# A 64-batch stack of six attentions, an expert layer and a Mamba block on one core: the exponential moved behind the transpose, own scores copied out by ScalarE, and the expert fetches split

## The reference

```python
# L0: x += attn(ln(x), own, causal); x += attn(ln(x), ctx); x += gelu(ln(x) @ fc1) @ fc2
# L1: x += attn(ln(x), own);  x += attn(ln(x), ln(ctx));  x += top-2-of-8 experts(ln(x))
# L2: x += mamba2(rms(x));    x += attn(ln(x), ctx, mask_keys)
# L3: x = ln(x + attn(x, ctx, mask_pairs))
s = jnp.einsum('blhd,bmhd->bhlm', q, k)
p = jax.nn.softmax(s, axis=-1)
return jnp.einsum('bhlm,bmhd->blhd', p, v)
```

## Time and profile before

| what | value |
|---|---|
| median of 3 runs | 3734.92 us (3720.77 to 3736.32) |
| the profiled execution's own time | 3734.74 us |
| its span | 3732.9 us |
| PE busy | 3195.7 us, 86% |
| PEld busy | 2269.6 us, 61% |
| DVE busy | 2605.4 us, 70% |
| ACT busy | 2652.3 us, 71% |
| POOL busy | 1246.9 us, 33% |
| mean granted clock of PE | 0.952 |

### The profile page before, as it was taken

The page is one execution under the profiler, slowest core; times in us unless marked ns, Lnnn a source line. Parts: engine busy times, 40 slices in busy tenths (PEclk is TensorE's granted clock), DMA queues, the critical chain, the costliest instruction groups (busy, mean ns, idle before and its releaser), DMA issues.

```text
span 3732.9 us, 87645 instructions
## 1 busy us (share of the span) xinstructions
PE 3195.7 (86%) x30064; PEld 2269.6 (61%) x30064; DVE 2605.4 (70%) x5408; ACT 2652.3 (71%) x5088; POOL 1246.9 (33%) x1615
## 2 busy tenths in 40 slices
PE   6898888888888979998988888998888997777897
PEld 3566556566756657665665656666565665665565
DVE  7877787755477777556888777665888877326775
ACT  4777777777876757887776766788776776656566
POOL 3122333212153353112244244212235434214632
PEclk9999999999999989999999999999999998989899
DMA  7013200134410033221000014322000004442000
GB/s 280 1 43 135 109 6 15 30 97 108 103 37 3 18 100 89 69 64 43 19 22 14 3 44 109 83 72 57 26 23 20 6 19 108 103 112 59 16 2 13
DMA packets 211920, 212.98 MB, mean 57 GB/s; under 512 B 51808, under 2 KB 155168, under 8 KB 211232
## 3 DMA queue, kind: packets, MB, share of 16 engines
q1 hardware_dynamic: 203296, 190.58, 18.1%
q0 software_dynamic: 8192, 16.79, 1.5%
HBM read 135.98 MB, written 71.30 MB: 56 GB/s over the span
## 4 chain that ended last, share of the span: by engine, by line
PE 39%; DVE 23%; ACT 15%; issue 8%; SPq 7%; DMA 4%; POOL 4%; ACTq 0%; DVEq 0%; POOLq 0%
PE ps L1933 8%; DVE mx L2320 6%; PE ps L1923 5%; PE ps L1945 4%; DVE pr L2326 4%; DMA b_up<-cols 4%; ACT block_hid L2211 3%; ACT pt L2164 3%; PE ps L1892 3%; PE ps L1953 2%; PE ps L2005 2%; PE ps L1918 2%; DVE kx L2326 2%; ACT xh L2114 2%; SPq L1818 1%
## 5 line engine op out<-in xcount | busy, mean ns | idle before, releaser
L2320 DVE TENSOR_REDUCE mx<-ps 128x8 f32<-128x616 f32 (+1 forms) x704 | 671.4, 954 | 334.7 <-PE ps L1923 316.4
L2164 ACT ACTIVATE pt<-ps 77x512 f32<-77x512 f32 (+1 forms) x1408 | 768.9, 593 | 126.1 <-PE ps L1933 123.2
L2576 POOL TENSOR_TENSOR kx<-kT,in_tiles 128x308 f32<-128x308 f32 (+1 forms) x384 | 315.7, 822 | 830.5 <-PE ps L1923 740.0
L1933 PE MATMUL ps<-k_sb,pr 128*77 128x128 f32 (+1 forms) x3776 | 538.9, 284 | 33.9 <-ACT pr L2155 10.3
L1933 PEld LDWEIGHTS ps<-k_sb,pr 128*77 128x77 f32 (+1 forms) x3776 | 421.1, 147 | 142.2 <-issue 73.2
L1945 PE MATMUL ps<-pt,v 77*16 77x128 f32 (+2 forms) x11264 | 444.3, 278 | 29.0 <-ACT pt L2164 11.2
L2326 DVE TENSOR_TENSOR pr<-ps,mx 128x616 f32<-128x616 f32 (+1 forms) x472 | 450.3, 954 | 16.2
L2155 ACT ACTIVATE pr<-pr 128x616 f32<-128x616 f32 (+1 forms) x472 | 392.7, 840 | 75.6 <-DVE pr L2326 74.6
L2173 ACT ACTIVATE og<-ps 128x256 f32<-128x256 f32 x704 | 267.3, 381 | 236.8 <-PE ps L1945 233.6
L1923 PE MATMUL ps<-kx,qT 32*128 32x308 f32 (+2 forms) x2816 | 361.6, 547 | 42.2 <-ACT pt L2164 15.8
L1945 PEld LDWEIGHTS ps<-pt,v 77*16 77x16 f32 (+2 forms) x11264 | 251.8, 97 | 181.1 <-issue 85.1
(11 more groups left out here) (209 smaller groups left out, 5733.3 us busy)
## 6 DMA issues: line engine op xcount, KB each, us to landing
w_up<-weights SPq DMA_DIRECT2D x160, 256.0 KB
w_down<-weights SPq DMA_DIRECT2D x160, 256.0 KB
sent<-block_hid SPq DMA_DIRECT2D x42, 512.0 KB, 6.3
made<-block_hid SPq DMA_DIRECT2D x42, 512.0 KB, 6.3
block_rows<-sent SPq DMA_DIRECT2D x160, 64.0 KB
b_down<-expert_b SPq DMA_DIRECT2D x160, 64.0 KB
made<-block_out SPq DMA_DIRECT2D x160, 64.0 KB, 2.2
cT<-ctx_cols SPq DMA_DIRECT2D x32, 154.0 KB, 3.1
```

The source lines that it names most:

```text
L1933: i = tr(p[0:keys, j * L:(j + 1) * L], probs[s][pl.slot(unit, 3)][:, c:c + keys], ident)
L2164: go_act(pt[s][0:keys, q % 2, :], p[0:keys, :], ACT.Copy).then_inc(probsT_ready.sem, 1)
L2320: link(v_.tensor_reduce(m, tile, AX.X, ALU.max, negate=True))
L2576: tell(pool, g_.tensor_tensor(spread_keys[s][:, pl.slot(step, 2), 0:4 * keys].rearrange("p (h k) -> p h k", h=4), kT[s][:, b * keys:(b + 1 ...
```

## The change

Three things change in what runs, and a fourth in the order.

1. In all attentions the exponential is taken off `soft`. The shifted scores are transposed, and ACT's copy from PSUM to `pt` becomes an exponential (L2376 in the changed file). The instruction on 8x77 or 8x128 elements in SBUF (L2155) is gone.
2. In the two own attentions (`LIFTED = (0, 2)`) a step `lift` stands ahead of `soft`: ACT copies the unit's scores out of PSUM (L2366), DVE takes the maximum from SBUF. `soft` is then on POOL: scores plus negated maximum in place (L2811). In the context attentions DVE's two instructions stay.
3. Of a pair of expert blocks the rows are fetched by a step of their own (`fetch`, L2013), the first weights for each block apart (`take`, with j), each with its own semaphore; the second bias has its own semaphore too. `block_turn` of the next pair waits for the rows alone, and stands ahead of this pair's `block_down`. The register loads stand ahead of the waits. `b_up` has two buffers.
4. The planner's durations and all its preference tables are new, so all engines' orders differ.

```diff
@@ attention_steps, expert_steps
+            out += [("lift", a, s, *units[n])] if a in LIFTED else []
             out.append(("soft", a, s, *units[n]))
...
-    out = [("table", g), ("take", g, 0), ("take_down", g, 0)]
+    out = [("table", g), ("fetch", g, 0), ("take", g, 0, 0), ("take", g, 0, 1), ("take_down", g, 0), ("block_turn", g, 0)]
     for p in range(PAIRS):
-        out += [("block_turn", g, p), ("block_up", g, p, 0), ("block_up", g, p, 1)]
-        out += [("take", g, p + 1)] if p + 1 < PAIRS else []
+        more = p + 1 < PAIRS
+        out += [("fetch", g, p + 1)] if more else []
+        for j in range(2):
+            out += [("block_up", g, p, j)] + ([("take", g, p + 1, j)] if more else [])
+        out += [("block_turn", g, p + 1)] if more else []
         out.append(("block_down", g, p))
@@ parts, tables
     if kind == "soft":
-        return [(V, 2.52 if t.own else 1.67), (A, act(8 * keys, 0.5))]
+        return [(V, 2.52 if t.own else 1.67)]
-STAY = 0.6307
+STAY = 0
+LIFTED = (0, 2)
@@ SP
-                elif kind == "take":
+                elif kind == "fetch":
...
+                    at = [nc.sync.value_load(row_of[0:1, g, n:n + 1], min_val=0, max_val=2 * REGION - L) for n in (2 * p, 2 * p + 1)]
...
                     if former:
-                        sp.wait_ge(*up_made(*former, 1))
-                        sp.wait_ge(*up_ready(*former, 1))
...
+                        sp.wait_ge(*block_turned(*former))
+                    for j, row in enumerate(at):
+                        sp.dma_start(block_rows[:, j, :], sent[bass.ds(row, L), :]).then_inc(rows_fetched, 16)
+                elif kind == "take":
+                    g, p, j = step[1:]
...
+                    if former:
+                        sp.wait_ge(*up_made(*former, j))
+                    sp.dma_start(w_up[:, j, :], weights[:, bass.ds(e * FF + W_FC1, FF)]).then_inc(ups_taken[j], 16)
+                    sp.dma_start(b_up[:, p % 2, j, :], cols[:, bass.ds(e * FC + C_AT["L1_fc1_b"][0], FC)]).then_inc(ups_taken[j], 16)
@@ PE
-                    pe.wait_ge(blocks_taken, 6 * 16 * in_order(g, q))
+                    pe.wait_ge(rows_fetched, 2 * 16 * in_order(g, q))
...
                     pe.wait_ge(*block_ready(g, q))
+                    pe.wait_ge(ups_taken[j], 2 * 16 * in_order(g, q))
@@ ACT
-                elif kind == "soft":
+                elif kind == "lift":
...
-                    act.wait_ge(*scores_shifted(*args))
-                    v = probs[s][pl.slot(step, 3)][:, 0:8 * keys]
-                    go_act(v, v, ACT.Exp, scale=t.scale).then_inc(probs_ready.sem, 1)
+                    act.wait_ge(*scores_made(a, s, b))
+                    old = pl.earlier(unit, 3)
+                    if old:
+                        for q in range(2):
+                            act.wait_ge(*shifted_turned(*old[1:4], 2 * old[4] + q))
+                    lo = pl.banks["scores", a, s, b][2 * h]
+                    go_act(shifted[s][pl.slot(unit, 3)][:, 0:8 * keys].rearrange("p (c x) -> p c x", c=2),
+                           ps[:, lo:lo + 2, 0:4 * keys], ACT.Copy).then_inc(scores_lifted.sem, 1)
...
-                    go_act(pt[s][0:keys, q % 2, :], p[0:keys, :], ACT.Copy).then_inc(probsT_ready.sem, 1)
+                    go_act(pt[s][0:keys, q % 2, :], p[0:keys, :], ACT.Exp, scale=t.scale).then_inc(probsT_ready.sem, 1)
@@ DVE
+                elif kind == "lift":
...
+                    dve.wait_ge(*scores_lifted(*args))
...
+                    tell(dve, v_.tensor_reduce(mx[:, s % S, pl.slot(unit, 3), :],
+                                               shifted[s][pl.slot(unit, 3)][:, 0:8 * keys].rearrange("p (n k) -> p n k", k=keys),
+                                               AX.X, ALU.max, negate=True), maxima_ready, *args)
@@ POOL
+                elif kind == "soft":
...
+                    pool.wait_ge(*maxima_ready(*args))
+                    tile = shifted[s][pl.slot(step, 3)][:, 0:8 * keys].rearrange("p (n k) -> p n k", k=keys)
+                    tell(pool, g_.tensor_tensor(tile, tile, mx[:, s % S, pl.slot(step, 3), :].unsqueeze(2).broadcast_to([128, 8, keys]),
+                                                ALU.add), shifted_by_g, *args)
```

More of the change, by code:

```diff
@@ L237, in parts @@
     if kind in ("keep", "give", "take_down"):
-        return [(Y, 0.3 if kind != "take_down" else 0.5)]
-    if kind == "take":
-        return [(Y, 1.2)]
+        return [(Y, {"keep": 0.3, "give": 0.6, "take_down": 0.8}[kind])]
+    if kind in ("fetch", "take"):
+        return [(Y, 0.5)]
     if kind == "clear":
@@ new lines @@
+     "hidden": {A: -2.979, P: 17.184}, "keep": {Y: -13.0834}, "lift": {A: -3.4607, V: -5.5393},
+     "load": {Y: -18.2249}, "mamba_out": {P: 7.2578, V: 6.6268}, "mix": {A: 1.128},
+     "mlp": {P: -3.4522, V: -5.4408}, "norm": {P: -0.2497}, "out": {V: 1.9482}, "pairs": {P: -5.374, V: -25.6452},
+     "project": {A: 1.451}, "regroup": {P: 8.5033, V: 0.4201}, "reload": {Y: 49.0198, V: 23.3143},
+     "rope": {P: -0.2343, V: -19.3769}, "route": {A: -5.4407, P: 8.0211, V: 14.6117},
+     "rows": {P: 14.2185, V: -1.6459}, "scan": {G: 1.5005, P: 3.425, V: -0.3541}, "scatter": {G: -10.5486},
@@ new lines @@
+    {"STAY": 0.6307, 4: -0.433, "bias": {G: -17.4648}, "block_down": {V: 0.196}, "clear": {Y: -46.383},
+     "combine": {V: -26.1409}, "context": {Y: -19.8314}, "count": {P: -0.0178}, "decay_in": {G: 42.8661},
+     "fetch": {Y: -21.1471}, "final": {A: -0.7708}, "gate_norm": {G: 38.106},
+     "gate_stats": {G: -2.3269, V: 27.9077}, "gates": {V: -22.1572}, "give": {Y: -2.3745}, "hidden": {P: 14.0646},
+     "load": {Y: -20.1077}, "mamba_out": {P: 0.0283, V: 8.1382}, "mlp": {V: 1.0382}, "norm": {P: -0.0085},
+     "out": {V: 0.2267}, "pairs": {V: -4.0768}, "regroup": {P: 19.6395}, "reload": {V: 19.228},
+     "rope": {P: -0.0306, V: -1.0088}, "route": {P: 9.3605}, "rows": {P: 7.0714}, "scan": {G: 4.3113, P: 0.0625},
+     "scores": {P: 6.2901}, "stats": {V: -0.1266}, "step_size": {V: 40.4033}, "store": {G: 2.7232, Y: -28.4414},
+     "table": {V: 28.0474}, "take": {Y: -20.557}, "turn_out": {A: -0.5592}, "values": {P: 59.1055},
+     "z": {P: 0.3065}},
@@ new lines @@
+    {"STAY": 0.6307, 1: -0.1333, 5: -0.4554, "bias": {G: -17.992}, "bias_mlp": {G: 38.8992},
+     "block_down": {V: 0.196}, "block_turn": {A: 0.2529}, "block_up": {A: -0.3646}, "clear": {Y: -46.383},
+     "combine": {V: -26.1409}, "context": {Y: -21.1068}, "count": {P: -0.0178}, "decay_in": {G: 43.0562},
+     "fetch": {Y: -21.1471}, "final": {A: -0.7708}, "gate_norm": {G: 35.133},
+     "gate_stats": {G: -2.3269, V: 27.9077}, "gates": {V: -22.1572}, "give": {Y: -0.8007}, "hidden": {P: 14.0646},
+     "load": {Y: -20.1077}, "mamba_out": {P: -0.4232, V: 7.6867}, "mlp": {V: 1.0382}, "out": {V: -0.1622},
+     "pairs": {V: -2.0672}, "regroup": {P: 19.6395}, "reload": {Y: 48.9647, V: 19.7824},
+     "rope": {P: -0.0306, V: -1.0088}, "route": {P: 9.509}, "rows": {P: 7.0714},
+     "scan": {G: 4.2786, P: 0.0021, V: -0.305}, "step_size": {V: 40.4033}, "store": {G: 2.7232, Y: -28.5809},
+     "table": {V: 28.0474}, "take": {Y: -21.1471}, "take_down": {Y: 13.2159},
+     "turn_gate": {A: 25.8648, P: -0.9198}, "values": {P: 61.2529}},
@@ new lines @@
+    {"bias": {G: -17.4648}, "block_down": {V: 0.196}, "block_turn": {P: 0.6254}, "block_up": {A: -7.2594},
+     "clear": {Y: -46.383}, "combine": {V: -26.1409}, "count": {P: -0.0178}, "decay": {P: -1.0004},
+     "decay_in": {G: 42.1653}, "fetch": {Y: -21.1471}, "final": {A: -0.7708}, "gate_norm": {G: 35.133},
+     "gate_stats": {G: -2.3269, V: 27.9077}, "gates": {V: -22.1572}, "gather": {G: -13.0928}, "give": {Y: -2.3745},
+     "hidden": {P: 13.6566}, "load": {Y: -20.1077}, "mamba_out": {P: 0.0283, V: 8.1382}, "mix": {P: -0.5795},
+     "mlp": {V: 1.0382}, "norm": {A: -0.1715, P: -0.1715}, "out": {V: 0.0143}, "pairs": {V: -1.8147},
+     "regroup": {P: 19.6395}, "reload": {Y: 55.1556, V: 21.5404}, "rope": {P: -0.0306, V: -1.0088},
+     "route": {P: 7.357}, "rows": {P: 7.0714}, "scan": {G: 4.3113}, "scatter": {G: -7.6381},
+     "spread": {G: -1.5363}, "step_size": {V: 40.4033}, "store": {G: 2.7232, Y: -28.4414}, "table": {V: 27.9892},
+     "take": {Y: -21.1471}, "values": {P: 61.2529}},
```

1763 lines of the change are left out of this document (964 added, 799 removed).

## The result

The changed kernel takes 3868.54 us (median of 4 runs, 3855.85 to 3876.99), the kernel before 3735.62 us in the same comparison (3720.77 to 3741.24): a ratio of 1.0359 (95% interval 1.0318 to 1.0401), slower by 3.6% where 4.5% faster was forecast.

The account below looks back on a forecast made before the run. PE was taken as nearest to full, with gains only in its 537 us of idle and the clock. 3732.9 - 80 (fetches) - 75 (hand-offs) - 15 (clock) = 3562.9, plus 1.8 around it: 3565 us; 8-in-10 range 3460 to 3690.

Parts of the forecast that it names:

- What bounds the kernel: Whole kernel: PE nearest full, 3195.7 of 3732.9 us busy; gain only from 537 us idle and clock; largest wait 108.2 us.
- Fetches apart: Expert pairs: requesting rows early nearly removes `block_turn`'s 108 us DMA wait; 80 us gained, between 40 and 108.
- the clock: Granted clock, 0.952 on the mean, partly recovers as PE's waits are filled: 15 us gained, between 0 and 30.
- SP's limit of 11.0 us a pair: Last expert group: SP's DMA issue needs 11.0 of 14.25 us a pair, so at most some 64 us come from there.
- the fetches give nothing: Rival on expert fetches: SP's occupied queue moves the wait from `block_turn` to `block_up`; 3660 us, chance 0.05.
- Hand-offs: Waits between engines, from 429 us of other idle: less DVE and ACT work gains 75 us, between 0 and 160.
- An exponential costs what the copy costs, and the count of table loads stays 239: ACT's copy to `pt` in attentions: exponential 0.593 us against copy 0.597, so no cost; table loads unchanged.
- Own units: Own attentions: chain 4.14 us instead of 3.50, one more hand-off; 164 us if cover is gone; DVE loses 313 us.
- POOL rival: POOL's in-order queue holds up own units, 430 us of lateness, a third on PE's path: 3797 us, chance 0.10.
- ACT's busy time: ACT over the whole kernel: 2652 us minus 318 for context exponentials and 7 for own units, 2327 us.
- the markers: Signs of success: engine busy times, DMA wait under 28 us, idle some 380, clock over 0.955, pairs 11 to 12 us.
- The last group still at 14 us a pair: Sign of being wrong: the last expert group's pairs not falling from about 14 us to 11 to 12 us.

Follow-up runs that it names:

- order of before: Parts of the change put into the kernel before's finished order, with its planner, tables and durations kept; fetches alone 0.9687, all three parts 1.0044.
- fetch ahead: Changed kernel with only SP's order edited: fetch of the next pair stands ahead of this pair's `take_down`; 3750.80 us, 1.0065 (0.9912 in another comparison).

## Why the prediction was wrong, step by step

With the kernel before at 3728 us the ratios make a chain:

| step | ratio to before | us | forecast |
|---|---|---|---|
| fetches apart, order of before | 0.9687 | -117 | -80, and -15 of clock |
| exponential behind the transposes | 0.9815 | +48 | part of -75 |
| own units over ACT, DVE, POOL | 1.0044 | +85 | part of -75 |
| the changed order, fetch ahead | 1.0065 | +8 | not priced |
| the fetch behind `give`, with `block_turn` ahead of `block_down` | 1.0369 | +113 | not priced |

*What bounds the kernel* was right: the largest wait was the fetch, and it was the one that paid.

*Fetches apart: in the changed order this step failed, and with it the sum.* The sum said that the rows are asked for "right behind the pair before's `block_turn`, ahead of its two `block_up`", and that "from the request to the use lies at least a `block_up` and what the order puts between". Neither is so: SP's order has the fetch behind `take_down` and `give`, and I did not look at it. The front part's rows of PE's order show `block_turn` ahead of `block_down`. The two together gave `block_turn` 161.9 us of waits where 28 were allowed. With the fetches alone, in the order of before, the request is as late, and the wait is gone since `block_down` lies ahead of the use. There the part gives 117 us, not 95. Idle time fell from 537 to 466 us, 71 us (forecast 80), and PE's busy time by 53 us through the clock, 0.952 to 0.969, where 15 were allowed: the clock was mis-sized. SP's limit of 11.0 us a pair held; 11.6 was reached. The rival "the fetches give nothing" looked at that queue, at `take` and `give` waiting behind one another, was given 0.05, and stopped at no gain. It should have been followed through to a price: 5.8 us of SP and 2.5 us of landing, with a `block_down` held up behind them and the next `take_down` behind that.

*Hand-offs, -75 us: the step failed, and with the wrong sign.* The slope was read from windows with different work. Taking 462 us of busy time from ACT gave nothing by itself (1.0074 with the exponential alone). In these orders ACT at 70% wasn't a limit; the term took its load for one, and left out what a later or longer item keeps waiting behind it.

*"An exponential costs what the copy costs, and the count of table loads stays 239".* Both statements are true in the changed order, and both missed the cost. In the order of before the count rises to 265 and the part costs 48 us; without the experts' gelu that cost is gone, at least in the stretch shown. The Trainium skill ("ScalarE: Activation LUTs", Rules for kernel authors) says to group functions by table set and do all of one set before switching; by it splitting one exponential into two among gelu is a step the wrong way, and the runs agree (0.9687 without, 0.9815 with). Its cost of a switch, about 2.7 us with a drain, isn't what the traces show: 1.283 us, and the next instruction 0.01 us behind (the median before). How large this cost is in the changed order, with its 239 loads, wasn't measured apart.

*Own units, +85 us.* The prediction gave the chain 0.64 us more a unit, 164 us "if the cover is gone", and took none of it. About half of it arose (85/256 = 0.33 us a unit; 53 us on the other chips), with DVE's 306 us of relief against it. The mechanism of the POOL rival was thus right in kind (its third of 430 us was 144, more than was measured). Its total of 3797 us was nearer than the forecast, but by luck: it keeps the 80 us of the fetches, which the changed kernel doesn't gain. Its marker was wrong: I had looked for more than 60 us of PE waiting for L2811, where the changed kernel has

```profile
L2138 PE MATMUL ps<-k_sb,pr 128*77 128x128 f32 (+1 forms) x3776 | 542.0, 286 | 31.3 <-POOL pr L2811 7.9
```

7.9 us there, and 5.4 us more for the third place, `kx`. A wait is put down to what ended last; a late unit shows as many small waits of others (over the rows of that view, PE's waits for ACT rise from 230 to 314 us from the fetches alone to all three parts, those for POOL from 12 to 54, and those for DVE fall from 142 to 93). The Trainium skill's advice to keep work of two inputs on VectorE ("GPSIMD Engine Reference", section 4.1) was weighed as a question of POOL's load. The row says 1.898 us against 1.224, 1.55 times and not two; but in the chain of a unit the advice held here, where halving POOL's instruction gave 39 us back, and no load figure shows that.

*ACT's busy time* was forecast at 2327 and is 2394 us. The removed exponentials' durations add up to 591 us, but ACT's consecutive instructions overlap: before, their sum is 3022 us in 2652 us of busy time. Taking the exponentials out, with 26 loads (33 us) more, freed only 462.

*Of the markers*, DVE near 2290, POOL near 1730 and L2811 under 2.1 us held. The DMA wait under 28 us (161.9), the idle time of 380 us (633.5), the clock above 0.955 (0.932) and 11 to 12 us a pair (14.5) did not; with the fetches alone, the wait, the clock and the pairs do. "The last group still at 14 us a pair" is the one sign of being wrong that came true.

## What to carry to other kernels

When a request and its use are steps in two engines' fixed orders, look at both orders: a request that stands late in its queue does little harm while ready work lies ahead of the use, and a consumer that is moved ahead of that work turns the late request into a stall of everything behind it. Either end can be moved. Busy time taken from an engine that isn't the bound bought nothing by itself here; price a longer chain and each additional table switch, and don't take them for covered because the engine has room. And run the parts of a change one by one in one frozen order: here one of three parts was worth 3.1%, and the other two together took 3.6% away.

## What the runs showed that was not expected

The kernel before was timed in six comparisons: 3735.6, 3729.2 and 3727.5 us in three, 3893.2, 3880.4 and 3882.2 us in the other three, 4% more, each comparison on one chip, and at one level throughout. In the trace of a run at the upper level the lag behind the lower one grows in steps of up to some 20 us and hardly between them, and a kind of wait appears that this group of instructions doesn't have at the lower level. ACT's group of copies after `mix` at the upper level:

```profile
L2173 ACT ACTIVATE og<-ps 128x256 f32<-128x256 f32 x704 | 266.8, 381 | 333.7 <-PE ps L1945 244.9 <-remote 84.3 <-issue 1.5
```

and the same group before at the lower one has 236.8 us of idle time, nearly all for PE, and no remote. "remote" is another core or a queue that the profile doesn't know; 3% of the chain that ended last are its. Many of the longer stalls lie where POOL issues indirect DMAs one behind another. What it is was not tested. It isn't the same for all kernels: fetch ahead is 0.9912 there and 1.0065 at the lower level, all parts 0.9953 and 1.0044, the changed kernel 1.0215 and 1.0369, but the exponential with the fetches 0.9817 and 0.9815. A ratio is to be compared only with one of the same level.

The granted clock nearly followed PE's idle time at the lower level: 0.969 at 466 us of idle, 0.959 at 488, 0.952 at 537 (the kernel before), 0.951 at 552, 0.954 at 557 and 0.936 at 632. It added 53 us to the 71 us of idle time that the fetches took out.
